# Twelve pad blocks from two queues, and scatters that wait for the one before last

## The reference

```
ys = geglu(xf @ Ws1 + bs1) @ Ws2 + bs2              # shared expert, for all 4096 tokens
logits = (xf @ Wr + br) / 1.5
top_val, top_idx = top_k(logits, 2)                 # two of 12 experts for each token
top_w = softmax(top_val)
h = xf @ We1[e] + be1[e]                            # each expert: 128 -> 768 -> geglu -> 384 -> 128
yE = geglu(h) @ We2[e] + be2[e]
x = layernorm(x + ys + sum over the two of top_w * yE)
```

## Time and profile before

| | us |
|---|---|
| median of 3 runs | 450.01 |
| lowest, highest | 448.95, 451.0 |
| span of the profiled execution | 471.4 |
| mean granted TensorE clock in it | 0.947 |
| busy: PE, DVE, ACT, POOL | 399.7, 312.4, 295.7, 256.0 |
| scatters, line 403: 64, 990 ns each | 63.4 |

### The profile page before, as it was taken

One profiled execution on the slowest core, in us unless ns is written; L12 is line 12 of the kernel. 1 busy time (PEld: TensorE's weight loads), 2 busy tenths in 40 slices (PEclk: granted clock), 3 DMA queues, 4 the chain that ended last, 5 costly groups with the idle time before them and its releaser, 6 DMA issues.

```text
span 471.4 us, 9935 instructions
## 1 busy us (share of the span) xinstructions
PE 399.7 (85%) x2503; PEld 307.2 (65%) x2503; DVE 312.4 (66%) x1065; ACT 295.7 (63%) x715; POOL 256.0 (54%) x328
## 2 busy tenths in 40 slices
PE   0566799998978988988593799999999999999991
PEld 0224466756746564664240369999999999999830
DVE  3799989999997997724560345656666665666162
ACT  2586699989796865663310237677777776777055
POOL 5666747567567857875566004444444444444264
PEclk9978799999999999997977699999999999999997
DMA  5389700000003000110122257876777776763394
GB/s 152 90 192 375 231 1 0 2 1 1 2 6 108 32 19 31 41 49 24 48 66 65 79 176 252 286 248 245 259 249 259 241 261 237 261 230 126 102 333 124
DMA packets 51471, 64.86 MB, mean 138 GB/s; under 512 B 8924, under 2 KB 35292, under 8 KB 51416
## 3 DMA queue, kind: packets, MB, share of 16 engines
q1 hardware_dynamic: 46968, 54.85, 35.1%
q0 software_dynamic: 4448, 9.38, 6.1%
HBM read 21.65 MB, written 13.91 MB: 75 GB/s over the span
## 4 chain that ended last, share of the span: by engine, by line
PE 51%; DVE 20%; issue 8%; SPq 6%; ACT 5%; POOL 4%; DMA 2%; another core or an unknown queue 2%; DVEq 0%; ACTq 0%; POOLq 0%
PE bank L1280 21%; PE bank L1298 11%; PE bank L987 4%; DVE rec L555 3%; DVE bst L475 2%; PE bank L969 2%; SPq L1087 2%; SPq L1086 2%; ACT z L690 2%; PE bank L1272 2%; PE bank L998 2%; PE bank L999 1%; PE bank L920 1%; POOL frs L821 1%
## 5 line engine op out<-in xcount | busy, mean ns | idle before, releaser
L1141 POOL DMA_INDIRECT routed_rows<-yo,goes_to x75 | 71.8, 957 | 112.8 <-DVE yo L1190 110.4
L1280 PE MATMUL bank<-xT,w 128*128 128x128 f32 x900 | 113.3, 276 | 0.6 <-ACT xT L1228 0.4
L1280 PEld LDWEIGHTS bank<-xT,w 128*128 128x128 f32 x900 | 106.6, 192 | 1.1 <-ACT xT L1228 0.5
L1182 DVE SCALAR_TENSOR_TENSOR actT<-bank,tile_bias,gl 128x128 f32<-128x128 f32 x225 | 65.3, 345 | 24.8 <-ACT gl L1234 15.1
L403 POOL DMA_INDIRECT dispatched_rows<-rows_all,slot_i x64 | 63.4, 990 | 22.7 <-issue 17.4
L1234 ACT ACTIVATE gl<-bank,tile_bias 128x128 f32<-128x128 f32 x225 | 65.9, 364 | 14.1 <-PE bank L1280 7.6
L1298 PE MATMUL bank<-we_sb,actT 128*128 x450 | 62.9, 276 | 1.0 <-DVE yo L1190 1.0
L1298 PEld LDWEIGHTS bank<-we_sb,actT 128*128 128x128 f32 x450 | 56.1, 192 | 1.6 <-issue 1.4
L1190 DVE SCALAR_TENSOR_TENSOR yo<-bank,goes,wb 128x128 f32<-128x128 f32 x75 | 26.3, 350 | 37.5 <-PE bank L1298 34.5
L1228 ACT ACTIVATE xT<-bank 128x128 f32<-128x128 f32 x75 | 20.8, 277 | 26.2 <-PE bank L1272 24.2
L969 PE MATMUL bank<-xk,wfk_sb 128*128 128x512 f32 x64 | 33.0, 626 | 4.9 <-DVE xk L572 3.8
(11 more groups left out here) (201 smaller groups left out, 778.4 us busy)
## 6 DMA issues: line engine op xcount, KB each, us to landing
w<-we_sb SPq DMA_DIRECT2D x75, 384.0 KB
x_all<-dispatched_rows SPq DMA_DIRECT2D x75, 68.0 KB
we_sb<-we SPq DMA_DIRECT2D x1, 4608.0 KB
rows_all<-x SPq DMA_DIRECT2D x8, 256.0 KB, 2.9
x_all<-routed_rows SPq DMA_DIRECT2D x8, 256.0 KB, 4.9
rows_all<-routed_rows SPq DMA_DIRECT2D x8, 256.0 KB, 5.3
out<-x_all SPq DMA_DIRECT2D x8, 256.0 KB, 2.5
routed_rows<-yo,goes_to POOLq DMA_INDIRECT x75
```

The costliest lines, as they stand in the source:

```text
L1141: ng.indirect_dma_start(routed, bass.IndirectOffsetOnAxis(ap=goes_to[n // U % DB][:, n % U:n % U + 1], axis=0), yo[n % YO][:, :], None).th ...
L1182: nv.scalar_tensor_tensor(actT[n % UA][:, at], ps_a[j][:, 0:P], tile_bias[:, j, n:n + 1], gl[n % 2][:, at], ALU.add, ALU.mult).then_inc(s2 ...
L1280: return nt.matmul(to[:, 0:P], w1[m][:, off:off + P], xT[m][:, :], start=True, stop=True)
```

## The change

ScalarE gets a step `place_pads` between `shared_gelu(4, 0)` and `shared_gelu(4, 1)`. It waits for `rows_known` and writes the six odd pad blocks; SyncE keeps the six even ones. The scatters now count on two semaphores, `dispatched` for the first choice and `dispatched_odd` for the second. From scatter 44 of 64 on (`PACED`), the scatter of tile n and choice k waits until all earlier ones of choice k have landed, so that at most two are under way. SyncE waits for both semaphores before its row loads.

```diff
+    PACED = (BATCH[-1][0] * CT - CT + 2) * K
...
+                if i >= PACED:
+                    g.wait_ge(s[("dispatched", "dispatched_odd")[k]], n * 16)
                 ng.indirect_dma_start(dispatch, bass.IndirectOffsetOnAxis(ap=slot_i[:, k, n:n + 1], axis=0), rows_all[:, n, :],
-                                      None).then_inc(s["dispatched"], 16)
+                                      None).then_inc(s[("dispatched", "dispatched_odd")[k]], 16)
...
+            def place_pads():
+                a.wait_ge(s2["rows_known"], 1)
+                for n in range(1, E, 2):
+                    to = a.value_load(pad_at[0:1, n:n + 1], min_val=0, max_val=E * REGION - P)
+                    na.dma_start(dispatch[ds(to, P), :], pad_rows[n * P:(n + 1) * P, :]).then_inc(s2["pads_placed"], 16)
...
-            shared_gelu(4, 0); shared_gelu(4, 1); shared_gelu(5, 0)
+            shared_gelu(4, 0); place_pads(); shared_gelu(4, 1); shared_gelu(5, 0)
...
             sp.wait_ge(s2["rows_known"], 1)
-            for n in range(E):
+            for n in range(0, E, 2):
...
-            sp.wait_ge(s["dispatched"], SLOTS // P * 16)
+            sp.wait_ge(s["dispatched"], NT * 16)
+            sp.wait_ge(s["dispatched_odd"], NT * 16)
             sp.wait_ge(s2["pads_placed"], E * 16)
```

More of the change, by code:

```diff
@@ L252, in build @@
                   "logits_psum logits_ready rows_zero expert_w_loaded bias_loaded iotas "
-                  "pads_built pads_written route chosen fall_ready rel_ready prefix_ready slots_ready dispatched").split():
+                  "pads_built pads_written route chosen fall_ready rel_ready prefix_ready slots_ready dispatched dispatched_odd").split():
             s[n] = sem(n)
```

## The result

The changed kernel took 452.06 us in the median of 16 runs (450.59 to 453.39), the kernel before 450.0 us in 16 runs beside it (448.95 to 451.49): ratio 1.0047, 95% interval 1.0033 to 1.0060, some 2.1 us slower. A median counts all runs, while a ratio leaves out slow ones, over 1.5% above the fastest of their kernel; this comparison has none. The forecast was 455.0, within 446 to 460: the sign came out as forecast, the size was under half of it.

The account below looks back on a forecast made before the run. Three chains from the last slots to the first expert tile were to decide: ScalarE's pads hold up the shared expert, +3.5 us, half clock +1.9, pacing 0. That made 455.4, said as 455, within 446 to 460 us.

Parts of the forecast that it names:

- stray waits: Late engine starts around the last routing batch, marked "remote"; 23.9 us in the profile, claimed mostly absent from timed runs.
- rival 1: Waits around the last scatters are in timed runs too and pacing removes them: 434 to 442 us; chance 0.15.
- T: End of the CAST that writes the last routing batch's slots; three chains to the first expert tile start there.
- T + 28.8: When SyncE's pads and weight loads were said to let TensorE go on in the kernel before, undisturbed.
- The pads: Six pad blocks on ScalarE, 1.27 us each, 7.6 in all, delay the next gelu to T + 8.1.
- shared chain: Rest of the shared expert through TensorE, ScalarE and VectorE (DVE): T + 22.8 before the change, T + 28.4 after.
- the half clock: TensorE at 0.50 clock after some 5.5 us idle in the shared expert: 0 to 3.2 us, taken as +1.9.
- The pacing: Late scatters' wait for earlier ones to land, claimed met 0.6 us ahead and put at 0.
- Rival 4: Every paced scatter waits for a late landing: 459 us, deciding from 1.5 us a scatter on; chance 0.05.
- rows' chain: Last batch's scatters on POOL, then SyncE's row loads for the first expert tile; scatters forecast over at T + 21.1.
- The sum: Whole kernel: 3.5 for the held-up chain plus 1.9 for clock makes 5.4 on 450.0, forecast 455.
- term of +3.5: ScalarE's pads hold up the shared expert, so TensorE goes on at T + 32.3 against T + 28.8.

Follow-up runs that it names:

- pads only: Changed kernel without the pacing wait: 452.0 us, 1.0034 of the kernel before at its 450.45 us level; 0.9944 to 0.9994 on slower occasions.
- pacing only: Changed kernel with all twelve pad blocks back on SyncE: 452.63 us, 1.0066 of the kernel before at its 450.45 us level; 0.9831 to 0.9875 on slower occasions.

## Why the prediction was right and wrong

**The stray waits: taken out rightly, for a wrong reason.** The step said they were "mostly there under the profiler alone". They aren't: a run's time is its span plus 1.7 to 1.8 us, with the waits and without. They belong to the occasion, or its chip. The comparison happened to be of the level without them, so it was luck that the sum on 450 was of the right kernel; on an occasion like that of the profile, rival 1's case held in sign (0.9909), with 4 us of gain in place of its 10. Their size ahead of T was low as well: 4.0 + 4.7 = 8.7 us forecast, 32.2 - 21.55 = 10.7 measured. A span 21 us over the median said that profile and times didn't belong together; it didn't say why. The rule that was weighed there, of the Trainium skill (NOTIFIC — the notification-queue block, 7.1 Overflow), would have the record path hold back its producers. No run here shows that: nearly every run on record has a span and so was recorded, which means that its share in the waits of one level can't be excluded. But the step that rested on it, waits in the profile and none in the timed runs, is refuted.

**The chain that failed: "T + 28.8".** The scatters were put at 0.28 after T, as in the rows, but there T came 12 us later, and POOL had run dry. With the waits out T moves up to 223 to 226, the scatters before it don't, and POOL reaches the last batch 3.1 to 3.4 us after T (pads only and the changed kernel; 3.75 in pacing only). So unpaced scatters end at T + 22.1, not T + 19.2. From pads only the row loads then start at T + 25.0; pacing only shows 1.95 us from there to PE's first product on the rows (252.05 to 254.00). The kernel before would have its rows at T + 27.0. With the shared expert's last second product at T + 23.2 (pacing only), that chain has 3.8 us to spare, not 2.1. Both are read from kernels beside it, since the kernel before has no profile of this level.

**The pads: right in kind, 1.3 us low.** Forecast with the clock: gelu at T + 8.1, shared chain's end at T + 28.4 + 1.9 = T + 30.3. Pads only has the gelu at T + 8.7 and the end at T + 31.5, the changed kernel T + 8.5 and T + 31.6. Six pads from ACT take 6.7 us, where 1.27 each had given 7.6. The second product starts at T + 10.8 (changed) and T + 11.1 (pads only), not T + 9.8, since it waits for DVE's sum (L617) too. From there to the end it is 20.7 us in the changed kernel and 20.4 in pads only, against 18.2 in pacing only, where PE has no such wait: the half clock costs 2.2 to 2.5, where the term was 1.9.

**The pacing: put at 0, but not free.** The wait "met 0.6 us ahead" is not: 1.49 to 1.51 us a scatter, the last at T + 26.0 in place of T + 22.1. Rival 4 had this; it had put the point from which it decides at 1.5. There it stands: in the changed kernel the rows' chain and the shared chain end within 1 us, so pacing added little to the pads: the first `actT` at T + 35.1 in place of pads only's T + 34.0. The long gaps (1.53 and 1.85) stand in 240 to 248, around the end of the five weight loads of 384 KB, and that these delay the landings is likely. They are not the whole of it: in pacing only a gap of 1.28 stands at 231.60, 9 us ahead of the weight loads. No run took this apart.

**The sum.** In the same measure, the end of the shared chain against the rows' coming, the forecast was T + 30.3 against T + 28.8 - 3.9 = T + 24.9: 5.4 us. The runs give T + 31.5 against T + 27.0: 4.5. So the step that failed is the term of +3.5 for six pads on ACT, counted against a kernel before that goes on at T + 28.8: its rows' chain was 2.1 us too short there, the held-up chain 1.3 (clock included). Another part is the clock of the first gate: after a wait for the rows it took 2.90 us in pacing only, 1.58 in the changed kernel. If the kernel before pays that too after its 3.8 us of waiting, which no profile shows, it gives the change back some 1.5 us: 3.0. Measured were 2.1 for the change and 1.5 for pads only; for pacing only it is 4.0 (T + 31.0 against T + 27.0) and 2.2 to 3.0 measured, by the medians and by the ratio. What shrank the cost is thus the slack of the shared expert, that is the unpaced rows' chain against which every cost was counted; and I had given the kernel before no loss of clock. About 1 us beyond both stays open. A candidate is in the profile of pacing only: there a scatter issued at T + 21.2 landed 1.1 us late (3.69 against 2.56), under weight loads that end at T + 23.3. The kernel before has the same pads and weight loads on SP, and its last scatter at T + 22.1 would fall under them, so its row loads would start about 1.1 us after T + 25.0. This is an estimate; no trace of the kernel before at this level shows it. Why an occasion is of one level or the other stays open too.

Of what was to show in the profile, ACT's six DMAs, PE's idle time after one product, the half clock behind it, and SP through its weight loads (243.25) before the last scatter (251.66) came as said; scatters 1.26 apart did not. The prediction has SP through its weight loads by T + 16.4, though its own terms give 8.1 + 5.7 = 13.8; it was T + 17.6, in any case ahead of the last scatter.

## What to carry to other kernels

Compare the profiled execution's time with the timed runs before working out anything; where they differ by per cents, measure both versions again on one occasion, and note the chip, rather than explaining the gap away. When waits are taken out of a profile and an event moves earlier, ask of each engine queued on it whether it would be free by then. Two delays on parallel chains that end together don't add, and undoing one of them gives little back.

## What the runs showed of the hardware

- On some occasions a row of indirect scatters, 1.26 us apart, comes with other engines starting 4 to 14 us late and stretches SP's first six pads to 22 us (7.3 without). The whole kernel is then 22 to 25 us (5%) slower; in the profiles 10.7 us of it lie between PE's product at 205 us and T, and 8.4 to 9.6 between T and the first `actT`. On others the same program has none of it.
- Where it occurs, a full wait at every fourth scatter takes the waits away (-1.8%; beside pads on ACT one of 4.6 us was left, -1.0%). At every sixth some are back, for -2.3%, within the interval of the other.
- A scatter of 128 rows takes POOL 0.96 us, follows the one before it by 1.26 us, and by 2.56 us if it waits for that one to land. With each waiting for the one before last, beside pads and weight loads, they follow by 1.5 on average (1.49 and 1.51).
- After 6.3 and 7.8 us of idle time PE ran at half clock (0.50): a second product took 3.75 us in place of 1.88, twelve gate products 2.90 in place of 1.58.
